# First map of the second feed-forward: fp32 or half-precision parts for batches 0 to 5

## The reference, cut to what matters

```python
def _qlora_linear(x, q, scale, bias, la, lb):
    w = _dequant(q, scale)
    base = jnp.einsum('btd,od->bto', x, w) + bias
    lora = jnp.einsum('btr,or->bto', jnp.einsum('btd,rd->btr', x, la), lb)
    return base + lora
...
h = x
for blk in range(3):
    i0, i1 = (2 * blk, 2 * blk + 1)
    y = _qlora_linear(h, qweights[i0], scales[i0], biases[i0], lora_a[i0], lora_b[i0])
    y = _layernorm(y, ln_gamma[blk], ln_beta[blk])
    y = jax.nn.gelu(y, approximate=False)
    y = _qlora_linear(y, qweights[i1], scales[i1], biases[i1], lora_a[i1], lora_b[i1])
    h = y + h
...
x = x + 0.5 * _L0_ffn_ref(_layernorm(x, axis=-1), ...)
x = x + _L0_attn_ref(_layernorm(x, axis=-1), ...)
x = x + 0.5 * _L0_ffn_ref(_layernorm(x, axis=-1), ...)
```

## Time and profile before

| | |
|---|---|
| three runs | 972.86 us median (972.62 to 973.87) |
| the profiled execution | 972.9 us, of it 971.1 us span |
| TensorE busy | 961.8 us, 99% |
| TensorE weight load | 515.7 us, 53% |
| VectorE, ScalarE, GpSimd busy | 854.1, 812.1 and 839.3 us |
| attention (slots) | about 98 to 907 us of the span |

### The profile page before, as it was taken

How to read it: one execution, slowest core, us unless ns; L and a number is a source line. 1 busy time by engine, 2 the same in 40 slices (tenths; PEclk the granted TensorE clock), 3 DMA queues, 4 the chain that set the end, 5 groups by cost and what they waited for, 6 DMA issues and landing times.

```text
span 971.1 us, 19647 instructions
## 1 busy us (share of the span) xinstructions
PE 961.8 (99%) x6077; PEld 515.7 (53%) x6077; DVE 854.1 (88%) x1738; ACT 812.1 (84%) x1366; POOL 839.3 (86%) x961
## 2 busy tenths in 40 slices
PE   8999999999999999999999999999999999999998
PEld 8777444444444444444444444444444444444777
DVE  7879988999999998999899999999999998986666
ACT  6886888888988898888888888888888898889774
POOL 4776798999998999899989999999999998899553
PEclk9999999999999999999999999999999999999999
DMA  9001322222222222222222222222222222221003
GB/s 239 21 1 45 88 66 62 59 63 62 57 63 63 66 66 66 67 66 63 59 61 63 59 61 66 66 66 67 66 66 61 56 66 59 61 62 34 1 1 88
DMA packets 72162, 59.92 MB, mean 62 GB/s; under 512 B 11328, under 2 KB 70976, under 8 KB 72064
## 3 DMA queue, kind: packets, MB, share of 16 engines
q1 hardware_dynamic: 71280, 58.18, 24.5%
q10 hardware_dynamic: 784, 0.53, 0.2%
HBM read 6.23 MB, written 2.10 MB: 9 GB/s over the span
## 4 chain that ended last, share of the span: by engine, by line
PE 95%; DVE 4%; issue 0%; ACT 0%; POOL 0%; DVEq 0%; ACTq 0%; POOLq 0%
PE ps L1444 12%; PE ps L1445 11%; PE ps L1446 11%; PE ps L1436 11%; PE ps L1437 11%; PE ps L1429 7%; PE ps L1316 4%; PE ps L1420 3%; PE ps L1463 3%; PE ps L1459 3%; PE ps L1460 3%; PE ps L1422 3%; PE ps L1421 3%; PE ps L1345 3%; PE ps L1326 2%; PE ps L1360 1%
## 5 line engine op out<-in xcount | busy, mean ns | idle before, releaser
L542 POOL TENSOR_TENSOR p_lo<-work_b,p_hi 128x1024 f16<-128x1024 f32 x256 | 539.8, 2129 | 44.3 <-ACT p_hi L731 42.3
L1087 DVE TENSOR_REDUCE mcol<-ps 128x2 f16<-128x1024 f32 x256 | 301.4, 1221 | 1.3 <-PE ps L1429 1.0
L726 ACT ACTIVATE work_b<-ps,exp_scale 128x1024 f32<-128x1024 f32 x256 | 271.6, 1110 | 33.2 <-PE ps L1437 32.9
L731 ACT ACTIVATE p_hi<-work_b 128x1024 f16<-128x1024 f32 x256 | 256.4, 1055 | 0.6 <-ACT work_b L726 0.4
L1444 PE MATMUL ps<-p_hi,xn_hi 128*128 128x512 f16 x512 | 194.8, 380 | 0.0
L1436 PE MATMUL ps<-head_ops 128*128 128x512 f16 x512 | 194.1, 379 | 0.5 <-DVE mcol L1087 0.3
L1445 PE MATMUL ps<-p_hi,xn_lo 128*128 128x512 f16 x512 | 194.0, 379 | 0.0
L1446 PE MATMUL ps<-p_lo,xn_hi 128*128 128x512 f16 x512 | 194.0, 379 | 0.0
L1437 PE MATMUL ps<-head_ops 128*128 128x512 f16 x512 | 194.0, 379 | 0.0
L551 POOL TENSOR_TENSOR x<-x,o_sb 128x512 f32<-128x512 f32 x126 | 159.9, 1269 | 5.3
L1098 DVE STREAM_TRANSPOSE head_ops<-mcol 32x128 f16<-32x128 f16 x512 | 155.4, 304 | 9.3
(11 more groups left out here) (169 smaller groups left out, 1411.5 us busy)
## 6 DMA issues: line engine op xcount, KB each, us to landing
head_ops<-pair_ops SPq DMA_DIRECT2D x512, 64.0 KB, 2.0
head_ops<-pair_ops SPq DMA_DIRECT2D x128, 128.0 KB, 2.4
x<-x_dram SPq DMA_DIRECT2D x8, 256.0 KB, 5.7
out<-x SPq DMA_DIRECT2D x7, 256.0 KB, 3.1
vo_last<-wvo_dram SPq DMA_DIRECT2D x1, 1024.0 KB, 12.2
qk<-wq_dram SPq DMA_DIRECT2D x1, 512.0 KB, 3.9
qk<-wk_dram SPq DMA_DIRECT2D x1, 512.0 KB, 5.0
qw<-qweights_dram SPq DMA_DIRECT2D x1, 256.0 KB, 5.8
```

The source lines that it names most:

```text
L542: pool.tensor_tensor(p_lo[:, k % 2, rows, :], p32[:, k % 2, rows, :], p_hi[:, k % 2, rows, :], ALU.subtract).then_inc(plo_done, 1)
L726: nc.scalar.activation(p32[:, k % 2, 2 * a:2 * a + 2, :], s_ps[a], ACT.Exp, scale=exp_scale[:, 0:1]).then_inc(exp_done, 1)
L731: nc.scalar.activation(p_hi[:, k % 2, 2 * a:2 * a + 2, :], p32[:, k % 2, 2 * a:2 * a + 2, :], ACT.Copy).then_inc(phi_done, 1)
L1087: nc.vector.tensor_reduce(mcol[:, pair % 2, :, t, 0], max_ps[pair == 1][t % 2], AX.X, ALU.max, negate=True).then_inc(max_red, 1)
```

## The change

For batches 0 to 5 the map is taken in half-precision parts, high and low. The last row of the weights is subtracted from all the others, which changes nothing since the features add up to zero, and the bias takes its place: row 127 of the stationary side is set to one in the high part and zero in the low part, so that the product adds the bias. `fold_first` makes that weight (`w1`), `first_weight_scaled` multiplies it by a power of two (`inv2[:, 3]`) and the constant under the root by its square (`eps1`), ScalarE and GpSimd make `w1_hi` and `w1_lo`. The tokens' parts `hx_hi` and `hx_lo` lie where `qk32` and `vo_last` were, which nobody reads any longer by then. In the slots of `late` ScalarE copies the transposed half twice, to `hT` and to `hx_hi`, and VectorE subtracts (`low_half`). The matmuls for a batch are 12 of 128 columns in f16 in place of 1 of 512 columns in bf16 and 4 of 128 in fp32.

```diff
     STEPS = NB * UNITS
-    NTOP = 3
+    NTOP = 4
+    HALF_UNITS = 3
+    HALF_B = 2 * HALF_UNITS
     LN_EPS = 1e-5
...
         gam = sb("gam", [128, NB])
+        w1 = sb("w1", [128, D])
+        w1_hi = sb("w1_hi", [128, D], F16)
+        w1_lo = sb("w1_lo", [128, D], F16)
+        minus_last = sb("minus_last", [128, 128], BF16)
+        eps1 = sb("eps1", [128, 1])
         bet = sb("bet", [128, NB])
...
         vo_last = sb("vo_last", [128, H, D])
+        hx_hi = qk32[:, :, :].rearrange("p a n -> p (a n)")[:, 0:HALF_B * T // 2].rearrange(
+            "p (b c) -> p b c", b=HALF_B).bitcast(F16)
+        hx_lo = vo_last[:, :, :].rearrange("p h d -> p (h d)")[:, 0:HALF_B * T // 2].rearrange(
+            "p (b c) -> p b c", b=HALF_B).bitcast(F16)
         w_hi = sb("w_hi", [128, 2, H * R], F16)
...
         bmean_ps = ps[:, 6, 0:NL]
+        fold_ps = ps[:, 7, 0:D]
         brow_ps = ps[0:3, 7, 0:(NB + 1) * D]
...
             pool.memset(mcol[:, :, :, :, :], 0.0).then_inc(prep_p, 1)
+            pool.memset(minus_last[:, 0:D - 1], 0.0)
+            pool.memset(minus_last[:, D - 1:D], -1.0).then_inc(minus_ready, 1)
+            pool.wait_ge(minus_ready, 1)
             pool.wait_ge(prep_p, 4)
...
                     clear_heads(i - 4)
+                if i == 8:
+                    pool.wait_ge(rstd_ready, 9)
+                    pool.memset(hx_lo[96:128, :, :], 0.0).then_inc(hx_clear, 1)
+                    pool.wait_ge(hx_clear, 1)
                 if i in (9, 10):
...
             vo_low(1)
+            pool.wait_ge(w1_high, 1)
+            pool.tensor_tensor(w1_lo[:, :], w1[:, :], w1_hi[:, :], ALU.subtract).then_inc(w1_low, 1)
+            pool.wait_ge(w1_low, 1)
+            pool.memset(hx_hi[96:128, :, :], 1.0).then_inc(hx_clear, 1)
+            pool.wait_ge(hx_clear, 2)
             xn_low(0, 0)
...
                 nc.scalar.activation(dst, src, ACT.Copy).then_inc(h0_ready, 1)
+                if b < HALF_B:
+                    act.wait_ge(hx_clear, 2)
+                    dst = hx_hi[0:D - 1, b, half_cols(h)].rearrange("p (a t) -> p a t", a=2)
+                    nc.scalar.activation(dst, src[0:D - 1], ACT.Copy).then_inc(hxh_ready, 1)
...
                     nc.scalar.activation(w_hi[:, n, :], qk32[:, n, :], ACT.Copy).then_inc(prep_a, 1)
+                if i == 10:
+                    act.wait_ge(w1_scaled, 1)
+                    nc.scalar.activation(w1_hi[:, :], w1[:, :], ACT.Copy).then_inc(w1_high, 1)
                 if i in (10, 11):
...
                     link(dve, nc.vector.tensor_reduce(amax[:, 2:3], vo_amax[:, :], AX.X, ALU.max))
-                    nc.vector.tensor_scalar(amax[:, 0:3], amax[:, 0:3], 1e-30, None, ALU.max).then_inc(prep_v, 1)
+                    nc.vector.tensor_scalar(amax[:, 0:NTOP], amax[:, 0:NTOP], 1e-30, None, ALU.max).then_inc(prep_v, 1)
...
                 dve.wait_ge(top_spread, 1)
-                nc.vector.tensor_copy(pow2[:, 0:3], top_cols).then_inc(pow_ready, 1)
+                nc.vector.tensor_copy(pow2[:, 0:NTOP], top_cols).then_inc(pow_ready, 1)
                 dve.wait_ge(pow_ready, 1)
-                link(dve, nc.vector.tensor_scalar(inv2[:, 0:3].bitcast(I32), pow2[:, 0:3].bitcast(I32), -1.0,
+                link(dve, nc.vector.tensor_scalar(inv2[:, 0:NTOP].bitcast(I32), pow2[:, 0:NTOP].bitcast(I32), -1.0,
                                                   ONE_BITS2, ALU.mult, ALU.add))
                 link(dve, nc.vector.tensor_scalar(inv2[:, 0:2], inv2[:, 0:2], QK_TOP, None, ALU.mult))
-                link(dve, nc.vector.tensor_scalar(inv2[:, 2:3], inv2[:, 2:3], VO_CLAMP, 1.0 / VO_CLAMP,
+                link(dve, nc.vector.tensor_scalar(inv2[:, 2:NTOP], inv2[:, 2:NTOP], VO_CLAMP, 1.0 / VO_CLAMP,
                                                   ALU.min, ALU.max))
...
                 dve.wait_ge(sq_ready, at(f, i, 1))
-                link(dve, nc.vector.tensor_scalar(u_var[:, q, :], sumsq[:, q, :], 1.0 / D, LN_EPS, ALU.mult, ALU.add))
+                if f == 1 and i < HALF_UNITS:
+                    dve.wait_ge(w1_scaled, 1)
+                    link(dve, nc.vector.tensor_scalar(u_var[:, q, :], sumsq[:, q, :], mean_mat[:, 0:1], eps1[:, 0:1],
+                                                      ALU.mult, ALU.add))
+                else:
+                    link(dve, nc.vector.tensor_scalar(u_var[:, q, :], sumsq[:, q, :], 1.0 / D, LN_EPS, ALU.mult,
+                                                      ALU.add))
                 nc.vector.tensor_scalar(u_rstd[:, q, :].bitcast(I32), u_var[:, q, :].bitcast(I32), -0.5, MAGIC,
...
                                         ALU.mult).then_inc(w_scaled, 1)
+
+            def fold_first():
+
+                dve.wait_ge(fold_done, 1)
+                link(dve, nc.vector.tensor_tensor(w1[:, :], wt[:, 0, :], fold_ps, ALU.subtract))
+                nc.vector.tensor_reduce(amax[:, 3:4], w1[:, :], AX.X, ALU.max,
+                                        apply_absolute_value=True).then_inc(w1_folded, 1)
+
+            def first_weight_scaled():
+
+                nc.vector.tensor_scalar(eps1[:, :], inv2[:, 3:4], inv2[:, 3:4], LN_EPS, ALU.mult, ALU.mult)
+                nc.vector.tensor_scalar(w1[:, :], w1[:, :], inv2[:, 3:4], None, ALU.mult).then_inc(w1_scaled, 1)
...
             seed(0, 1)
+            fold_first()
             dve.wait_ge(rest_scaled, 1)
...
                     weight_scaled(i - 7)
+                if i == 9:
+                    first_weight_scaled()
                 if i in (9, 10):
...
+            def low_half(m, h):
+                dve.wait_ge(hx_clear, 2)
+                dve.wait_ge(hxh_ready, 2 * m + h + 1)
+                lo, hi = [t[0:D - 1, m, half_cols(h)].rearrange("p (a t) -> p a t", a=2) for t in (hx_lo, hx_hi)]
+                nc.vector.tensor_tensor(lo, late_ps[0:D - 1], hi, ALU.subtract).then_inc(hxl_ready, 1)
+
             def late(k):
...
                     late_means(m)
+                for m, h in late_at(k, "ffn", "turn"):
+                    if m < HALF_B:
+                        low_half(m, h)
...
                 for c, b in [unit_batches(i)[c] for c in halves]:
+                    if f == 1 and i < HALF_UNITS:
+                        pe.wait_ge(w1_low, 1)
+                        pe.wait_ge(hxl_ready, 2 * b + 2)
+                        for t in range(TT):
+                            dst, cols = bank[f][b][:, t * D:(t + 1) * D], slice(t * 128, (t + 1) * 128)
+                            nc.tensor.matmul(dst, hx_lo[:, b, cols], w1_hi[:, :], start=True, stop=False)
+                            nc.tensor.matmul(dst, hx_hi[:, b, cols], w1_hi[:, :], start=False, stop=False)
+                            ins = nc.tensor.matmul(dst, hx_hi[:, b, cols], w1_lo[:, :], start=False, stop=True)
+                        ins.then_inc(lin1_done, 1)
+                        continue
                     if n == 0:
...
             lin1(0, 0)
-            keep_warm(10)
+            pe.wait_ge(minus_ready, 1)
+            nc.tensor.matmul(fold_ps, ident[:, D - 1:D].to_broadcast([128, 128]), wt[:, 0, :], start=True, stop=False)
+            nc.tensor.matmul(fold_ps, minus_last[:, :], bias_rows[:, 0, :], start=False, stop=True).then_inc(fold_done, 1)
+            keep_warm(8)
             pre(2)
...
             lin1(0, 2, [1])
+            pe.wait_ge(w1_folded, 1)
             pre(7)
...
+            def ffn_reader(m, h):
+                return (hxl_ready, 2 * m + h + 1) if m < HALF_B else (h0_ready, B + 2 * m + h + 1)
+
             def late(k):
...
                     pe.wait_ge(xff_a, 2 * m + h + 1)
-                    late_turn(k, x_tile(m), h, pre_t, h0_ready, B + 2 * m + h + 1)
+                    late_turn(k, x_tile(m), h, pre_t, *ffn_reader(m, h))
...
                 ring = k % 4
```

More of the change, by code:

```diff
@@ L194, in macaron @@
         h0_ready = sem("h0_ready")
+        minus_ready = sem("minus_ready")
+        fold_done = sem("fold_done")
+        w1_folded = sem("w1_folded")
+        w1_scaled = sem("w1_scaled")
+        w1_high = sem("w1_high")
+        w1_low = sem("w1_low")
+        hx_clear = sem("hx_clear")
+        hxh_ready = sem("hxh_ready")
+        hxl_ready = sem("hxl_ready")
         h_ready = sem("h_ready")
```

## The result

The changed kernel takes 974.93 us (median of 17 runs, 974.82 to 976.02), the kernel before beside it 972.79 (17 runs). The ratio is 1.0025, 95% interval [1.0019, 1.0032]: slower by 2.1 us, where 975.0 had been forecast.

What follows compares the result with a forecast made beforehand. TensorE was taken as the bound, busy 961.8 us of a span of 971.1. From 972.9 us, start +2.2, slots 0 and end -0.05 gave 975.0; its own range 974.3 to 975.8, the overall range 973.0 to 976.2.

Steps and rivals of the forecast that it cites:

- The clearing: GpSimd's clearing of hx_lo between newtons 8 and 9: 2.65 us, 2.75 with the wait for itself.
- Newton 10: GpSimd's newton 10 behind the clearing ends 2.2 us later: 2.75 less idle times of 0.17 and 0.38.
- the first `project`: TensorE's first instruction of attention begins 2.1 us later, and the shift stays to the end.
- the +0.1 for collisions: Shifted GpSimd and VectorE instructions hold each other up near w_lo: between -0.3 and +0.5 us, taken as +0.1.
- third rival: The clearing also blocks VectorE, newton 9 ends up to 0.7 us later: 975.6 us, chance 0.22.
- Second clearing, `w1_lo`: Between vo_low and xn_low, where GpSimd was idle for 3.86 us: 0.
- The map: Slot 127: 0.67 us a batch, 0.44 less; of the 1.75 for batches 0 to 3 at most 0.1 gained.
- The slots at 0: One more copy and subtraction in each of 12 slots, hidden: 0, upper bound 2.6 us.
- the 0 booked for the rounding of `w1_hi` on ScalarE: At the start, the rounding has idle time behind it: 0; all small start items together at most 0.3 us.
- Slot 127 at -0.05: Sum of the end, the map's cut turning into waits: -0.05 us, bounds -2.6 and 0.
- The end of the span: After batch 7's norm TensorE works without waiting, on instructions the change leaves alone.

Runs made afterwards that it cites:

- experiment 3: Kernel before with only the first clearing (3072 16-bit elements) added between newtons 8 and 9: 974.34 us against 972.35, ratio 1.0022.
- experiments 4, 6 and 7: Changed kernel with slot 127's map in fp32: 975.12 us; changed kernel with slot 127's transposes in another bank: 974.01; kernel before with that bank: 972.50.
- experiment 2: Changed kernel with both clearings in 32-bit words and the first moved behind vo_lo: 972.78 us against 972.35 for the kernel before, ratio 1.0002.
- experiment 8: Changed kernel with both clearings in 32-bit words behind vo_lo and slot 127's transposes in the projections' bank: 972.04 us against 972.52 for the kernel before.

## Why the prediction was right, step by step

- **The clearing**: 2.65 us forecast, 2.65 measured. Newton 10 was put at +2.2 and moves by 2.0 (experiment 3), the first `project` at +2.1 and moves by 1.9. The 0.2 too much stand at newton 9's first operation, which VectorE held up to 0.74 us before (66.40) and to 0.52 in experiment 3; the +0.1 for collisions was not found. Shown by doing it alone, cheaper, and elsewhere.
- **Blocked VectorE** (third rival): its mechanism is there, its price is not. The clearing holds `vo`'s scaling from 0.74 to 2.02 us. By the Trainium skill, "SBUF — State Buffer", section "Who interferes with whom", whoever issues first has the shared port pair for the whole instruction; the trace agrees here too. But the scaling ends while TensorE's input is still to come, and it delays newton 9 less than before.
- **Second clearing, `w1_lo`**: hidden, as forecast.
- **The map**: 0.67 us a batch, as forecast. Its cut ahead of the transposes became their wait (1.75), as forecast; experiments 4, 6 and 7 show it from three sides.
- **The slots at 0**: the copies and subtractions cost nothing, as forecast, but the slots lose 0.2 to 0.3 us (shift of `y_hi` in experiment 2: 0.05 at head 0, 0.32 at head 126). The step that missed is the 0 booked for the rounding of `w1_hi` on ScalarE because it has idle time around it: this one instruction ahead of the slots moves ScalarE's recurring losses to places where they cost more.
- **Slot 127 at -0.05**: it loses 0.27, since GpSimd's such loss fell into slot 124, from where on it has no idle time; its addition then delays VectorE's seed.
- So the sum up to batch 7's transposes was 1.9 + 0.25 + 0.27 = 2.4 us in the profiles (2.1 and 2.45 in the two sets of runs) and not +2.2 - 0.05. That the total came out at 975.0 is partly luck: two small misses, the start too dear and the rest too cheap.
- **The end of the span**, booked as unchanged: from the last matmul to the end, the landing of the last output transfer, are 3.84 us in the profile of the kernel before, 3.24 to 3.53 in the other four without the parts in the slots and 3.10 or 3.11 in all nine with them. Why is not shown, and the profile of the kernel before lies highest of all; it means that a few tenths of the loss at TensorE need not arrive in the time.

## What to carry to other kernels

A clearing is an instruction like any other: on GpSimd write it in the widest words its bytes allow (1.37 us in place of 2.65 here), and put it where its engine waits, not where its result is first thought of. A cut on the busiest engine is worth what the next wait there lets through; look for that wait's other end (here a PSUM bank shared with an output) and give it a place of its own. In a program that is tight to 0.3 us, compare engines' idle time instruction by instruction before a small loss is put down to the work that was added.

## What the hardware showed that was not expected

- GpSimd's clearing, which reads nothing, holds up VectorE's SBUF-to-SBUF `tensor_scalar` to its end (L1003: 2.02 against 0.74; L1050: 1.44 for 128 elements). One on a single element (L1049: 0.20, from 67.53 on, inside the clearing) is not held up. VectorE's `tensor_tensor` out of PSUM beside it is not held up (L986: 1.29 for two, as before).
- Each of ScalarE and GpSimd can lose 0.28 or 0.29 us at every 128th instruction of its program, where 8192 bytes of code are fetched next; at most of these places no late start shows, perhaps since it falls into idle time. One instruction more or less ahead moves the places. In all it decided some 0.5 us here. What it waits for stays open.
- The early 1.1 us in both profiles of the changed kernel go with TensorE's granted clock: it stays at its lower level (1.2 GHz; the upper is 2.4) for 6.83 us at a stretch there, in the other 12 profiles for 3.41 us or not at all. Work of the engines, with the number of their instructions, then the granted clock (0.50 and 1.00), from 7.73 to 14.56 us, in the changed kernel and in experiment 2:

```profile
7.73:14.56 6.83, 6.83 (x33) 6.61 (x33) 6.32 (x32) 4.39 (x19) 2.88 (x10) 0.50 1.05 231
...
7.73:14.56 6.83, 6.15 (x51) 5.54 (x50) 6.28 (x33) 6.12 (x24) 2.39 (x8) 1.00 0.94 227
```

TensorE (first pair) gets 33 matmuls in place of 51. Ahead of it TensorE had been idle for 1.11 us until 6.68, but experiment 8, which keeps the upper level, shows 1.24 us of the same; so what decides it stays open.
